# The front of a two-layer block in a new order on every engine: norm by block, a scale of its own for W_in's v half, u last, sums of W1 behind g

## The reference, cut to what matters

```python
def attn(x):                                  # D = 512, K = 3
    uv = x @ in_proj_w + in_proj_b            # [8192, 1024]
    u, v = uv[..., :D], silu(uv[..., D:])
    v = depthwise_conv3(v) + conv_b           # along the 8192 rows
    h_t = a * h_{t-1} + ssm_b * v_t           # scan; a = sigmoid(logit_a)
    y = ssm_c * h + ssm_d * v
    out = (u * silu(y)) @ out_proj_w + out_proj_b
    return layernorm(out + x) * ln_w + ln_b
def ffn(x):                                   # 512 -> 2048 -> 512
    h = gelu(x @ ternary(W1).T + b1)          # exact gelu
    return h @ ternary(W2).T + b2
x = x + layernorm(attn(layernorm(x)))
x = x + layernorm(ffn(layernorm(x)))
```

## Time and profile before

| | |
|---|---|
| median of 3 runs | 1473.19 us (1472.39 to 1473.97) |
| the profiled execution: its own time | 1474.28 us |
| its span | 1472.5 us |
| TensorE (PE) busy | 1420.7 us, 96% |
| VectorE (DVE) busy | 1119.5 us, 76% |
| ScalarE (ACT) busy | 874.7 us, 59% |
| POOL busy | 442.5 us, 30% |
| mean granted clock of TensorE | 0.986 |

### The profile page before, as it was taken

How to read it: one execution, slowest core, us unless ns; L and a number is a source line. 1 busy time by engine, 2 the same in 40 slices (tenths; PEclk the granted TensorE clock), 3 DMA queues, 4 the chain that set the end, 5 groups by cost and what they waited for, 6 DMA issues and landing times. The chain is left out here.

```text
span 1472.5 us, 18968 instructions
## 1 busy us (share of the span) xinstructions
PE 1420.7 (96%) x6511; PEld 641.2 (44%) x6511; DVE 1119.5 (76%) x1884; ACT 874.7 (59%) x1259; POOL 442.5 (30%) x510
## 2 busy tenths in 40 slices
PE   6879889999999999999999999999999999999997
PEld 4333334444444444444444444444444444444443
DVE  7788677796867878687787867779686777998634
ACT  6686556555656756565675656556565665653543
POOL 2124304142331514233151422415232251422211
PEclk9889999999999999999999999999999999999999
DMA  9511213121221213122121311211131131001200
GB/s 265 222 36 36 58 43 86 25 62 30 64 51 30 75 22 77 29 51 65 29 65 22 86 29 38 78 30 58 29 87 29 29 86 29 29 1 29 57 29 29
DMA packets 155520, 82.00 MB, mean 56 GB/s; under 512 B 132768, under 2 KB 132768, under 8 KB 155296
## 3 DMA queue, kind: packets, MB, share of 16 engines
q1 hardware_dynamic: 155424, 80.79, 21.5%
HBM read 31.49 MB, written 16.78 MB: 33 GB/s over the span
## 5 line engine op out<-in xcount | busy, mean ns | idle before, releaser
L575 PE MATMUL f2b<-w,ring 128*128 128x512 fp8e5 x1008 | 382.2, 379 | 4.9 <-DVE ring L720 3.0
L576 PE MATMUL f2b<-w,ring 128*128 128x512 fp8e5 x1008 | 382.2, 379 | 0.0
L547 PE MATMUL f1b<-x3T,w 128*128 128x512 f16 x960 | 367.4, 383 | 6.4 <-DMA x3T<-tp 4.5
L548 PE MATMUL f1b<-x3T,w 128*128 128x512 f16 x960 | 367.3, 383 | 0.0
L1203 ACT ACTIVATE ring<-f1b,par 128x512 f32<-128x512 f32 x256 | 174.8, 683 | 225.5 <-PE f1b L548 225.1
L720 DVE SCALAR_TENSOR_TENSOR ring<-ring,f_sc 128x512 f16<-128x512 f32 x256 | 209.8, 834 | 51.6 <-ACT ring L1213 51.6
L1506 POOL TENSOR_SCALAR ve<-mv 128x4 f32<-128x4 f32 (+2 forms) x85 | 31.2, 367 | 722.5 <-DVE mv L712 722.2
L1213 ACT ACTIVATE ring<-ring,f_sc 128x512 f16<-128x512 f32 x256 | 180.3, 710 | 0.0
L497 PE MATMUL misc<-x1T,win_hi 128*128 128x512 f16 x464 | 175.9, 379 | 3.7 <-DMA x1T<-tp 2.3
L498 PE MATMUL misc<-x1T,win_hi 128*128 128x512 f16 x464 | 175.9, 379 | 0.0
L499 PE MATMUL misc<-x1T,win_lo 128*128 128x512 f16 x464 | 175.9, 379 | 0.0
(11 more groups left out here) (210 smaller groups left out, 2034.7 us busy)
## 6 DMA issues: line engine op xcount, KB each, us to landing
out_dram<-hb SPq DMA_DIRECT2D x64, 256.0 KB, 2.0
xs<-x_dram SPq DMA_DIRECT2D x15, 1024.0 KB, 5.7
ring<-w1t_dram SPq DMA_DIRECT2D x3, 1024.0 KB, 8.2
xs<-w_in_dram SPq DMA_DIRECT2D x4, 512.0 KB, 7.4
stage<-w2t_dram SPq DMA_DIRECT2D x2, 1024.0 KB, 15.2
x1T<-tp SPq DMA_TRANSPOSE x68, 3.1
xs<-x_dram SPq DMA_DIRECT2D x4, 256.0 KB, 3.4
x3T<-w_out_dram SPq DMA_DIRECT2D x1, 1024.0 KB, 13.0
```

The source lines that it names most:

```text
L547: pe.matmul(b[:, :], w, src[:, k, :], start=k == 0, stop=False)
L548: mm = pe.matmul(b[:, :], w, src[:, KC + k, :], start=False, stop=k == KC - 1)
L575: pe.matmul(f2b[q][:, :], h_hi[:, i % H_SLOTS, qs], w2[:, j, :], start=j == 0, stop=False)
L576: mm = pe.matmul(f2b[q][:, :], h_lo[:, i % H_SLOTS, qs], w2[:, j, :], start=False, stop=j == FC - 1)
```

## The change

The front's lists are new on every engine:

- x: statistics, aggregation, reciprocal root (`rstd_first`, 3 linked instructions of POOL, one block each) and norm of tile 0 go block by block; tile 1 is loaded and normed in two halves. VectorE's first items are the parameters.
- W_in: it lies in `stage` now and is loaded as four pieces of 256 KB (the v half) and, between the transposes of tile 0, two of 512 KB (the u half). Each half has a scale of its own, from the sum over the partitions of the squared maxima: maxima by row, `win_square`, one small matmul with `ones`, and four linked VectorE instructions (`win_scale`). TensorE's matmul for the u half stands ahead of v of tile 0. The normed x of tile 2 lies in `stage` too.
- TensorE: 24 warming matmuls instead of 30; v of tile 0, v of tile 1, then u of tile 0, o of tile 0 block by block with `threshold(0)` ahead of the last block, v of tile 2, two groups of u of tile 1, the transposes of x3 with `threshold(1)` in the middle.
- The bias row of the out-projection: 4 VectorE additions (`add_bias`) into the residual instead of fp32 matmuls; `o_sc` and `out_bias` are gone.
- |W1|: all four sums on ScalarE, two of them after the last `gate_hi`. |W2|'s sums follow between the silus of tile 2.
- Signs: the first group of W2 is done by chunks in step 2 (`sign_first`), as are one quarter of W1 and two groups of W2. Ternary chunks 0 to 7 come ahead of step 2 (before: 0 to 8), some between the low parts of x3.
- ScalarE's tables for Silu and Gelu are loaded ahead of need by a one-column instruction (`load_table`).

```diff
+SIGNED = (1, 1, 1, 1, 2, 2, 2, 2, 3, 4, 5, 6, 7, 7, 7, 7, 8, 8, 8, 8, 9, 9, 9, 9)
+FIRST, SECOND = range(8, 21), range(28, 32)
+AT_TERNARY = {8: 1.19, 9: 2.25, 10: 3.3, 11: 3.5, 12: 5.11, 13: 5.12, 14: 5.7, 15: 5.75, 16: 6.3, 17: 6.4, 18: 6.6, 19: 7.4, 20: 7.6,
+AT_SIGN_C, AT_SIGN_Q, AT_SIGN_G = (0.5, 1.5, 2.5, 3.5), 4.4, (5.3, 6.5)
...
+        wf = stage.rearrange("p s n -> p (s n)").rearrange("p (k n) -> p k n", k=KC)
...
@@ sync: loads
-                sp.dma_start(wf[:, k, :], w_in_d[:, k, :]).then_inc(win_in[k], 16)
-            load_x(1)
+                sp.dma_start(wf[:, k, D:], w_in_d[:, k, D:]).then_inc(win_in[k], 16)
+            for i in range(2):
+                sp.dma_start(xs[:, 1, 2 * i:2 * i + 2, :], x_d[1, :, 2 * i:2 * i + 2, :]).then_inc(x1_in[i], 16)
+            for j in range(NB):
+                transpose("t1", 0, j)
+                if j < 2:
+                    sp.dma_start(wf[:, 2 * j:2 * j + 2, 0:D], w_in_d[:, 2 * j:2 * j + 2, 0:D]).then_inc(winu_in[j], 16)
             sp.dma_start(wo_raw, w_out_d).then_inc(wout_in, 16)
-            transposes("t1", 0)
+            load_x(2)
+            transpose("t1", 1, 0)
             load_w1(0)
+            for j in range(1, NB):
+                transpose("t1", 1, j)
             load_w1(1)
-            transposes("t1", 1)
-            load_x(2)
+            load_w1(2)
+            sp.dma_start(row[:, :, :], rows.partition_broadcast(P)).then_inc(row_in, 16)
             load_w1(3)
-            sp.dma_start(row[:, :, :], rows.partition_broadcast(P)).then_inc(row_in, 16)
-            load_w1(2)
-            load_w2(1)
             load_w2(2)
-            load_w2(0)
             load_w2(3)
             transposes("t1", 2)
+            load_w2(0)
+            load_w2(1)
...
@@ tensor: setup_in_proj
+                pe.wait_ge(x1_hi, 1)
                 warm(6)
                 pe.wait_ge(pmx, KC + 1)
+                pe.matmul(win_sum_bank(1), ones[:, :], wm_sq[:, 1, :], start=True, stop=True).then_inc(pm1, 1)
+                warm(6)
                 pe.wait_ge(x1_lo, 3)
+                warm(12)
+                pe.wait_ge(pmx, KC + 4)
+                pe.matmul(win_sum_bank(0), ones[:, :], wm_sq[:, 0, :], start=True, stop=True).then_inc(pm1, 1)
...
@@ tensor: the list
             for b in range(KC):
                 in_proj("v", 0, b, v_mm)
-            in_proj("u", 0, 0, u_mm)
-            in_proj("u", 0, 1, u_mm)
             for b in range(KC):
                 in_proj("v", 1, b, v_mm)
...
-            in_proj("u", 0, 2, u_mm)
-            in_proj("u", 0, 3, u_mm)
-            threshold(0)
-            o_first()
+            for b in range(KC):
+                in_proj("u", 0, b, u_mm)
+            for j in range(NB):
+                if j == NB - 1:
+                    threshold(0)
+                o(0, j)
...
@@ vector: new helpers
+            def add_bias(j):
...
+                ve_.tensor_tensor(hb[:, j, :], hb[:, j, :], ob_row, ALU.add).then_inc(ob_ok, 1)
+            def win_square(half_):
+                ve_.wait_ge(pmx, (KC + 3, KC)[half_])
+                ve_.tensor_tensor(wm_sq[:, half_, :], wm[:, half_, :], wm[:, half_, :], ALU.mult).then_inc(pmx, 1)
...
@@ vector: the list, x tile 0 and W_in
+            setup_params()
+            for j in range(NB):
+                x_stats(0, j)
+                aggr(0, 0, j)
+            win_max_v(0)
+            win_max_v(1)
+            t_lo("t1", 0, 0)
+            win_max_v(2)
+            t_lo("t1", 0, 1)
+            win_max_v(3)
+            win_square(1)
+            t_lo("t1", 0, 2)
+            win_scale(1)
+            t_lo("t1", 0, 3)
+            x_stats(1, 0)
+            setup_split(0)
+            x_stats(1, 1)
+            aggr(0, 1, 0)
+            aggr(0, 1, 1)
+            setup_split(1)
+            x_stats(1, 2)
+            setup_split(2)
+            x_stats(1, 3)
+            aggr(0, 1, 2)
+            aggr(0, 1, 3)
+            v_scale()
+            setup_split(3)
+            win_max_u(0)
+            win_max_u(1)
+            win_square(0)
...
@@ vector: the list, from the last gate on
+            gate(0, 3)
+            setup_out_proj(3)
+            gate_lo(0, 2)
+            gate_lo(0, 3)
+            t_lo("t1", 2, 0)
+            add_bias(0)
+            add_bias(1)
+            t_lo("t1", 2, 1)
+            add_bias(2)
+            h_add(0, 0)
+            add_bias(3)
+            threshold_sum(0)
+            t_lo("t1", 2, 2)
+            h_stats(0, 0)
+            h_add(0, 1)
+            t_lo("t1", 2, 3)
...
@@ vector: the last items ahead of step 2
+            first_norm(N3, pairs[0])
             threshold_sum(1)
...
+            ternary(0)
+            t_lo("t3", 0, 0)
+            t_lo("t3", 0, 1)
+            first_norm(N3, pairs[1])
+            ternary(1)
+            t_lo("t3", 0, 2)
+            t_lo("t3", 0, 3)
+            for o in range(2, 6):
+                ternary(o)
             threshold(1)
...
+            ternary(6)
+            ternary(7)
...
@@ scalar: the list, parts
             for j in range(NB):
                 front(0, j)
-            for i in range(2 * KC):
+            for i in range(KC):
                 split_in(i)
-            wo_square()
             for j in range(NB):
                 front(1, j)
...
             gate_hi(0, 2)
             gate_hi(0, 3)
+            abs_sum(2, 2, w1_raw[2], w1_in[2])
+            abs_sum(3, 3, w1_raw[3], w1_in[3])
+            t_hi("t1", 2, 2)
+            front(2, 3)
...
+            load_table(1, ACT.Gelu)
+            t_hi("t3", 0, 0)
...
@@ gpsimd
+            def rstd_first(j):
+
+                js = slice(j, j + 1)
+                rstd(0, 0, rs1[:, 0, js], False, js)
+                pool.tensor_scalar(nm1[:, 0, js], mean_var(0)[:, js, 0], rs1[:, 0, js], -1.0,
+                                   ALU.mult, ALU.mult).then_inc(front_rs, 1)
```

More of the change, by code:

```diff
@@ L209, in build @@
         win_in = [sem(f"win_in{k}") for k in range(KC)]
+        winu_in = [sem(f"winu_in{i}") for i in range(2)]
+        x1_in = [sem(f"x1_in{i}") for i in range(2)]
         w1_in = [sem(f"w1_in{q}") for q in range(4)]
@@ L505, in o @@
                 js = slice(j * P, (j + 1) * P)
+                if c == 0 and j == 0:
+                    pe.wait_ge(wo_l, KC)
                 for k in range(KC):
@@ L1020, in _ @@
+            u_bias()
+            x_stats(2, 0)
+            setup_split(KC + 1)
+            for j in range(1, NB):
+                x_stats(2, j)
+            for j in range(NB):
+                aggr(0, 2, j)
+            setup_split(KC + 2)
+            gate_scale()
             taps(0, 0, True)
             taps(0, 1, True)
-            gate_scale()
-            abs_sum(1)
+            setup_split(KC + 3)
             taps(0, 2, True)
+            wo_scale()
+            taps(0, 0, False)
@@ L1040, in _ @@
             taps(0, 2, False)
             y(0, 1)
-            threshold_sum(0)
+            taps(0, 3, False)
             setup_out_proj(2)
-            setup_out_proj(3)
+            scan(0, 2)
             ve_.wait_ge(par_ok, 8)
             gate(0, 0)
-            scan(0, 2)
-            taps(0, 3, False)
             y(0, 2)
+            gate(0, 1)
+            scan(0, 3)
+            ve_.wait_ge(g_sc_ok, 1)
             gate_lo(0, 0)
-            gate(0, 1)
-            threshold(0)
-            scan(0, 3)
@@ L1054, in _ @@
-            gate_lo(0, 1)
             y(0, 3)
             gate(0, 2)
+            gate_lo(0, 1)
             gate(0, 3)
+            setup_out_proj(3)
             gate_lo(0, 2)
             gate_lo(0, 3)
-            for j in range(NB):
-                ternary(j)
-                t_lo("t1", 2, j)
+            t_lo("t1", 2, 0)
[6 more added lines that the diff above has]
+            threshold_sum(0)
@@ L1063, in _ @@
+            t_lo("t1", 2, 2)
+            h_stats(0, 0)
+            h_add(0, 1)
+            t_lo("t1", 2, 3)
+            h_stats(0, 1)
+            aggr(1, 0, 0)
+            aggr(1, 0, 1)
+            h_add(0, 2)
+            threshold(0)
+            h_stats(0, 2)
             first = norms(0)
@@ L1378, in _ @@
                 front(0, j)
-            for i in range(2 * KC):
+            for i in range(KC):
                 split_in(i)
-            wo_square()
             for j in range(NB):
                 front(1, j)
-            for b in range(KC):
-                silu_v(0, b)
-                centre_tap(0, b)
+            split_in(KC)
+            split_in(KC + 1)
+            silu_v(0, 0)
+            wo_square()
+            split_in(KC + 2)
+            silu_v(0, 1)
+            split_in(KC + 3)
@@ L1430, in _ @@
+            load_table(1, ACT.Gelu)
+            t_hi("t3", 0, 0)
+            t_hi("t3", 0, 1)
+            copy_x3(0)
+            copy_x3(1)
+            copy_x3(2)
+            t_hi("t3", 0, 2)
+            t_hi("t3", 0, 3)
+            for n in range(3, len(halves_x3)):
+                copy_x3(n)
             for s in STEPS:
```

357 lines of the change are left out of this document (166 added, 191 removed).

## The result

| | before | after |
|---|---|---|
| median | 1473.58 us (1472.39 to 1473.98, 4 runs) | 1458.26 us (1457.15 to 1461.01, 4 runs) |
| ratio | | 0.990, 95% interval 0.9883 to 0.9917 |
| profiled execution: own time | 1474.28 | 1457.46 |
| its span | 1472.5 | 1455.7 |
| PE busy | 1420.7 | 1410.3 |

What follows compares the result with a forecast made beforehand. TensorE is full from 23.16 to 54.55 us, then waits, so the gain is `f1`'s earlier start: 16.2 - 0.9 - 1.0 for hand-overs = 14.3 us, giving 1460.0 profiled and 1458.9 median, range 1454 to 1465.

Steps and rivals of the forecast that it cites:

- Step 1: Start of the first tile: v(0) waits for the u half's maxima and starts at 23.3 us, as before (23.16).
- The clock's fall: TensorE idles some 3 us ahead of v(0), so its clock falls, which costs 2.7 us.
- The walk: The prediction's item-by-item timing of the engines up to `f1` and through step 2, with hand-overs taking no time.
- rival A: The clock does not fall ahead of v(0); of 2.7 us ScalarE's list lets 2.2 through: 1456.7 us, chance 0.27.
- Step 2 and 3: v(0), v(1), u(0) without a break, u(0) ending at 57.1 and ScalarE just fitting; o(0) starts at 58.8 (78.8 before).
- Step 4 and 5: Tile 2's transposes, then first layer norms, VectorE serial: v(2) at 70.7, `f1` at 92.4, 16.2 us earlier than before.
- Step 6: Step 2 of the pipeline: ScalarE's 4.3 us of added signs and chunks make `silu_y` late, losing 0.9 us.
- The sum: 16.2 - 0.9 = 15.3, less 1.0 for hand-overs: 14.3 us gained, 1460.0 profiled and 1458.9 median.
- the term for hand-overs: Some 12 hand-overs between engines on the path, which the walk left out, cost 1.0 us (0 to 3).

Runs made afterwards that it cites:

- a1: The kernel after with 24 more warming matmuls ahead of v(0): 1457.42 us, ratio 0.9898 to the kernel before.
- b4: The kernel after with the third and fourth sum of |W1| ahead of the first gate on ScalarE: 1462.83 us, ratio 0.9935 to the kernel before.
- b3: The kernel after with the out-projection's bias added on 4 of 512 columns only: 1458.00 us, ratio 0.9905 to the kernel before.
- a4: The kernel after with two sign blocks of W2 in step 2 taken of one column only: 1458.84 us, ratio 0.9908 to the kernel before.
- b2: The kernel after with ternary chunks 12 to 15 a little earlier among VectorE's items: 1456.44 us, ratio 0.9901 to the kernel before.
- c2: The kernel after with the rstd of x0 taken once for all four blocks: 1459.68 us, ratio 0.9919 to the kernel before.
- c3: The kernel after with W_in's v scale made after both halves' maxima, tile 1's norms ahead of the v splits: 1459.08 us, ratio 0.9915 to the kernel before.
- a3: The kernel after with 24 more warming matmuls and W1's first quarter loaded behind tile 1's transposes: 1454.85 us, ratio 0.9881 to the kernel before.
- c1: The kernel after with the edits of a3 and b2 and ScalarE's first |W1| sum behind `d_conv(0, 0)`: 1453.85 us, ratio 0.9877 to the kernel before.

## Why the prediction was right, and where it was not

**Step 1** held: the wait stood where it was put, behind VectorE's maxima of u, and the square was due at about 22.2, 1 earlier than walked, in part because W_in's first piece was there at 8.02 and not 8.6. POOL's power on 128x1 took 0.57 us, just below the bounds of 0.6 to 1.0, three of the four times, and 1.10, above them, the fourth.

**The clock's fall** held as an event (granted 0.78, v(0)'s first 14 starts 0.43 apart) but not as a cost. The walk ("v(0), v(1), u(0) without a break") left out that v(1) waits for tile 1's transposes: it looks at SP's queue for tile 2 but not for tile 1, and takes 3.2 to 4.1 us for a transpose where it took 6.4 amid three large loads. So rival A was mispriced: with the clock held (a1) o(0) starts 0.8 earlier, not 2.2, and 0.8 is within the range between executions. That v(1) came when the walk had it is luck in part: the term of 2.7 for the fall filled nearly the same time as the transposes, which would have held v(1) without it.

**Step 2 and 3.** o(0) at 59.47 instead of 58.8: v(0) started 0.65 earlier than walked, and v(1)'s wait, which costs 0.9 from start to start, and some small terms took that back and 0.7 more. ScalarE did fit, as forecast (19.71 of 21.12 us busy), and the moved sums and the lost bias matmuls did what was said; b4 shows what two of the sums would have cost in another place.

**Step 4 and 5** came out within 0.35. "VectorE is serial here" is true but not the whole: of 2 us taken off it only 0.3 come through, because TensorE and ScalarE are close behind (b3). The rule of the Trainium skill, "ScalarE: Activation LUTs" (What ACT_TABLE_LOAD costs), that some 1380 ns of drain come on top of a load, is not what this trace shows either: the instruction ahead of the load of 83.58 ends at 83.57, and the ACTIVATE behind it starts 1.29 us after it, at 84.87.

**Step 6** had the size and not the cause, so its hit is luck. 0.9 us were lost as forecast, and the first u gate came 33.8 after `f1`'s start, waiting for `silu_y`, as forecast too; but `silu_y` was late for ternary 15 on VectorE, not for ScalarE's added sign blocks (a4 against b2). With the chunks earlier the stretch is back at 52.15 (51.99 before), at nearly the same clock over the first 10 us of `f1` (0.71 and 0.72). I had counted that VectorE does the same number of ternaries, and had not asked when each is due.

**The sum.** 1460.0 was forecast for the profiled execution and 1457.46 measured: 0.3 from `f1`, 1.0 from the term for hand-overs, of which nothing is seen (`f1` came ahead of the walk, which had none), and 1.2 from the untouched rest. The median came nearer to its forecast (1458.26 against 1458.9) than the profiled execution did to its own (2.5 off), because the profiled execution lay 1.1 above the median that the forecast started from, and 0.8 below the median after. That closeness is luck.

What stays open: the order v(0), v(1), u(0), the removal of the bias matmuls, and what brings the 6.3 us between v(2) and `f1` (o(0) block by block, and `threshold(1)` behind the norms) were not tried by themselves; for these the account is read from the rows. The three parts tried make 2.7 + 2.4 + some 5 of the 16.5 us, if they add, which c2 and c3 may not, since both act by the same transposes.

## What to carry to other kernels

When a producer is made earlier, ask for the next consumer's own input before counting the gain: here v(0)'s start, the clock in v(0) and the order of the small matmul were each worth about nothing, because v(1)'s transposes landed when they did. Check also that a filler ends in time: the added warming matmuls held v(0) itself in a3 and c1. Large loads that are read later belong behind the small transfers that something waits for, and a sum over such a load belongs behind the work of its engine that is due first. Moving the same number of items is not neutral: look at the due time of each. And profile one program several times before a milestone is read to less than a microsecond: two executions of the same list were up to 2 us apart at v(1).
